# Low-rank weight products in one f16 pass, fewer weight maxima in batch 1, and four banks for its queries and keys

## The chip, the cores and the metric

The kernel runs on one core of a Trainium2 chip. The metric is the device time of one execution in microseconds (us). The engines work on queues of their own and meet at semaphores: TensorE (PE) multiplies matrices into the eight banks of PSUM, VectorE (DVE), ScalarE (ACT) and GpSimd (POOL) do the rest, and SyncE (SP) starts transfers.

## What is computed

The reference is two layers, each added to x (8 batches of 256 tokens, 512 wide).

```python
x = x + ffn0(attention0(x, cond))        # 16 heads; ffn 512 -> 2048 -> 512, relu
x = x + moe1(scan1(cond, x))             # 256 steps of an RK4 scan, then 8 experts, top 2, and a shared expert

w_up = (q - 7.5) * repeat(scale, 64)     # 4-bit codes, one scale for 64
y1 = x1 @ w_up + b_up + x1 @ lora_a @ lora_b        # lora_a [512,16], lora_b [16,2048]
y2 = relu(y1) @ w_down + b_down + relu(y1) @ lora_a2 @ lora_b2   # [2048,16], [16,512]
```

All inputs are f32 but the codes.

## The kernel before

`layer0` does batches 0 to 7 one after the other, `layer1` the scan and the experts. In layer 0 a batch has a stage of queries and keys (its values first), then four quads of four heads, then the product with `w_out`. From batch 2 on, PE does the FFN of batch b-2 in pieces between the attention products; batches 0 and 1 have none.

**Weights of the FFN (batch 0).** The 4-bit weights are made on the chip in 16 pieces of 128x1024 (`PIECES`). For piece h: SP loads codes and scales into one of three stages (it waits for `split` of piece h-3); DVE `unpack` multiplies codes and scales; PE `lora(h)` multiplies the low-rank factors, K = 16, two f32 products of 512 columns, into the banks `D[0]`, `D[1]`; DVE `correct(h)` adds them and counts `stage`; ACT `weights_high(h)` writes the f16 high part, POOL the low part (`split`). The low-rank correction is so folded into the weights. `lora(h)` waits for `stage` of piece h-1, since there is one pair of `D` banks. Pieces 0 to 3 go with the four chunks c of the query and key stage, pieces 4 to 15 with heads 0 to 11 (`lora(h + 4)` stands before `transposed(h)` on PE, `correct(h + 4)` and `unpack(h + 5)` before the copy of `turned(h)` on DVE). Ahead of all, DVE works out the scales (`weight_scales`) and multiplies the factors `lora_up`, `lora_dn` by them, which gives `lora_ok`. `unpack` and `correct` are in DVE's program order, so whatever DVE waits for there holds the head behind it.

**Maxima of the expert weights (batches 1 to 3).** The expert weights of layer 1 are split into f16 parts in batches 4 to 7, and the scale for this needs the largest of them. `part_max(n)` takes one piece of 128x512 (256 KB, loaded by SP into one of four buffers; the load of piece n waits for the maximum of piece n-4). There are 99 pieces, `max_parts(b, at)` deals them to the chunks (4 each) and heads of a batch: 33 to each of batches 1, 2 and 3.

**Queries and keys.** In chunk c PE writes them to `Gb[c % 2]` (banks 0 and 1); ACT squares them, PE sums the squares over a head (`head_norm`, banks `Rb`, 2 and 3), ACT makes 1/sqrt (Ln, Exp) and DVE writes the scaled result (`qk`, counted by `d_qk`). PE begins chunk c >= 2 when `d_qk` of chunk c-2 is there. Banks 6 and 7 (`D`) are idle in batch 1. In a quad PE makes the scores of four heads into banks 0 to 3 (waiting for the last copies, `d_pt`), DVE takes row maxima, ACT Exp, PE transposes, DVE copies back (`turned`), and the next quad's scores follow.

## Time and profile before

| | |
|---|---|
| time, median of 3 runs | 2954.64 us (2946.34 to 2957.25) |
| profiled execution, its own time | 2952.75 us |
| its span in the profile | 2951.0 us |
| PE, DVE, ACT, POOL busy | 95%, 59%, 38%, 46% |
| layer 0, the last largest value of a batch (L857) begins at | 871.3 us |

The busy shares are of the whole span, of which layer 0 is the first three tenths. A stage of layer 0 has its own limits, so the shares say little on this change; the stretches below are named by where they begin and end in us from the span's start.

### The profile page before, as it was taken

Reading aid. Unit: us, or ns where it says so; the run is one execution under the profiler, and the core shown is the slowest. Engines: PE = TensorE matmul, PEld = TensorE weight load, DVE = VectorE, ACT = ScalarE, POOL = GpSimd, SP = SyncE. Lnnn points to the kernel's source line nnn. Section 1 sums busy time; section 2 is a strip of 40 time slices with the busy share of each in tenths; the row PEclk is TensorE's granted clock in tenths of the full one; section 3 lists DMA queues with packets and bytes.
Section 4 is the critical chain, followed back from the end, with each engine's and each line's share of the span. In section 5 each row is a group of like instructions: output and inputs, shape, how many; then the busy total and the mean of one; then the engine's idle time right before and its main releaser. Section 6 shows DMA issues by size and latency. Waiting matters only on the chain.

```text
span 2951.0 us, 133155 instructions
## 1 busy us (share of the span) xinstructions
PE 2793.1 (95%) x49488; PEld 2435.4 (83%) x49488; DVE 1746.9 (59%) x6291; ACT 1125.3 (38%) x4986; POOL 1356.8 (46%) x3466
## 2 busy tenths in 40 slices
PE   7878998998898999999999999999999999999998
PEld 4355776776687778999998999999899899899987
DVE  4645564465464556666666666666666666666654
ACT  2332345456444433333333333333333333333322
POOL 2300001112115666666665666666566566566600
PEclk8578999999999998999999999999999999999999
DMA  7522233344430003444343443444444444344476
GB/s 245 148 79 93 68 106 129 124 147 140 144 100 3 3 4 111 130 129 134 126 130 122 129 131 119 139 129 125 124 130 128 128 130 125 119 138 125 125 232 199
DMA packets 137238, 361.02 MB, mean 122 GB/s; under 512 B 15888, under 2 KB 24720, under 8 KB 136592
## 3 DMA queue, kind: packets, MB, share of 16 engines
q1 hardware_dynamic: 136336, 354.17, 38.2%
q8 instruction: 158, 2.59, 0.4%
q10 hardware_dynamic: 672, 3.67, 0.3%
q14 instruction: 72, 0.59, 0.1%
HBM read 323.31 MB, written 34.47 MB: 121 GB/s over the span
## 4 chain that ended last, share of the span: by engine, by line
PE 59%; POOL 5%; issue 4%; DVE 1%; DMA 0%; ACT 0%; DVEq 0%; POOLq 0%; SPq 0%
PE pscan L1359 12%; PE pg L1264 12%; PE pd L1312 12%; PE pscan L1355 11%; PE pu L1264 11%; POOL lin L1109 1%; POOL lin L1125 0%; POOL from_q L1121 0%; POOL carry L1154 0%; POOL lin L1119 0%; POOL lin L1131 0%; POOL from_q L1127 0%; POOL from_q L1136 0%; POOL lin L1140 0%; PE prouter L1374 0%
## 5 line engine op out<-in xcount | busy, mean ns | idle before, releaser
L1355 PEld LDWEIGHTS pscan<-th,carry 128*128 128x128 f16 x16384 | 552.1, 96 | 73.8 <-ACT th L1174 52.8
L1355 PE MATMUL pscan<-th,carry 128*128 128x8 f16 x16384 | 560.6, 166 | 21.3 <-ACT th L1174 10.6
L1359 PE MATMUL pscan<-th,carry 128*128 128x16 f16 x16384 | 558.4, 169 | 2.2 <-DVE th L1470 1.4
L1359 PEld LDWEIGHTS pscan<-th,carry 128*128 128x128 f16 x16384 | 482.4, 96 | 3.4 <-DVE th L1470 3.3
L1174 ACT ACTIVATE th<-state 128x32 f16<-128x32 f32 x768 | 176.0, 229 | 714.0 <-DVE state L1487 714.0
L1264 PE MATMUL pg<-qh,wbuf 128*128 128x256 f16 x3168 | 432.0, 276 | 14.2 <-issue 14.2
L1312 PE MATMUL pd<-hg,wbuf 128*128 128x256 f16 x3168 | 429.5, 274 | 2.3 <-DMA wbuf<-w_split 2.3
L1264 PE MATMUL pu<-qh,wbuf 128*128 128x256 f16 x3168 | 426.9, 274 | 0.0
L1487 DVE TENSOR_REDUCE state<-pscan 128x32 f32<-128x96 f32 x768 | 197.6, 257 | 270.1 <-PE pscan L1359 264.8
L1264 PEld LDWEIGHTS pg<-qh,wbuf 128*128 128x128 f16 x3168 | 296.5, 98 | 53.9 <-issue 15.5
L1264 PEld LDWEIGHTS pu<-qh,wbuf 128*128 128x128 f16 x3168 | 294.3, 98 | 33.7
L1312 PEld LDWEIGHTS pd<-hg,wbuf 128*128 128x128 f16 x3168 | 278.2, 98 | 32.0 <-issue 2.6
L1482 DVE SCALAR_TENSOR_TENSOR pscan<-pscan,lin 128x32 f32<-128x32 f32 x1024 | 204.4, 200 | 125.1 <-POOL lin L1119 6.6
L1470 DVE TENSOR_TENSOR th<-pact,th 128x32 f16<-128x32 f32 x1024 | 190.7, 186 | 125.9 <-ACT pact L1175 122.8
L1142 POOL TENSOR_TENSOR from_q<-state,carry 128x32 f32<-128x32 f32 x256 | 91.1, 356 | 241.6 <-DVE state L1487 241.6
L1136 POOL TENSOR_TENSOR from_q<-state,carry 128x64 f32<-128x64 f32 x256 | 112.6, 440 | 164.9 <-DVE state L1487 164.9
L1174 ACT ACTIVATE th<-carry 128x32 f16<-128x32 f32 x256 | 58.6, 229 | 329.4 <-DVE carry L1487 323.2
L438 ACT ACTIVATE w_emb<-l0bank,nmax 128x256 f32<-128x256 f32 x256 | 118.8, 475 | 136.9 <-DVE nmax L812 136.9
L292 POOL TENSOR_SCALAR spare<-parts_mem 128x512 f16<-128x512 f16 x33 | 52.0, 1575 | 257.3 <-DMA w_split<-spare 163.6
L1239 ACT ACTIVATE hg<-hp 128x256 f16<-128x256 f32 x264 | 109.7, 416 | 136.3 <-DVE hp L1525 129.6
L310 POOL PARTITION_ALL_REDUCE fs<-fs x8 | 3.0, 378 | 327.3 <-DVE fs L857 327.3
L1525 DVE SCALAR_TENSOR_TENSOR hp<-hb,wk,gates 128x256 f32<-128x256 f32 x264 | 141.0, 534 | 18.7 <-DVE hb L1518 7.6
(231 smaller groups left out, 4928.5 us busy)
## 6 DMA issues: line engine op xcount, KB each, us to landing
wbuf<-w_split SPq DMA_DIRECT2D x264, 512.0 KB, 3.6
wbuf<-w_split SPq DMA_DIRECT2D x264, 384.0 KB, 3.1
parts_mem<-in_w_tiles SPq DMA_DIRECT2D x149, 256.0 KB, 3.1
w_split<-parts_mem SPq DMA_DIRECT2D x99, 256.0 KB, 2.8
late<-in_w_tiles SPq DMA_DIRECT2D x49, 256.0 KB, 3.2
w_split<-spare SPq DMA_DIRECT2D x33, 128.0 KB, 3.0
out<-oo SPq DMA_DIRECT2D x8, 512.0 KB, 3.7
xs<-in_x SPq DMA_DIRECT2D x1, 3584.0 KB, 14.8
```

What stands on the lines that cost most here:

```text
L438: ins = act.activation(pr[:, h % HPC, qc, :], X[h % HPC][:, qc * T:(qc + 1) * T], ACT.Exp, bias=nmax[:, h % HPC, qc:qc + 1], accum_out=psu ...
L1136: pl.tensor_tensor(ms3[:], rows(state[2][:], 2), c3[:], ALU.mult).then_inc(S["pchain"], 1)
L1174: act.activation(th[:, :, 0, :], v3(src[:]), ACT.Tanh, scale=unit).then_inc(S["th_ready"], 1)
L1239: act.activation(hg[:, slot, 0, :], hp[:], ACT.Identity, scale=2.0 ** -11).then_inc(S["hi_ready"], 1)
L1264: ins = mm(dst[:, 0:GT], wgu[:, slot, a, w, k, :], qh[:, q, k, :], start=(k == 0 and w == q), stop=(k == NC - 1 and w == 1))
L1312: ins = mm(pd[m // 2][:, (m % 2) * GT:(m % 2 + 1) * GT], wd[:, slot, w, m * P:(m + 1) * P], hg[:, slot, h, :], start=False, stop=False, sk ...
L1355: mm(pscan[:, 0, m * B:(m + 1) * B], clo[:, k, m * P:(m + 1) * P], th[:, k, 0, :], start=(m == 0 and k == 0), stop=False, skip_group_check ...
L1359: ins = mm(pscan[:, 0:2, m * B:(m + 1) * B], chi[:, k, m * P:(m + 1) * P], th[:, k], start=False, stop=(k == NC - 1), skip_group_check=True)
L1470: dve.tensor_tensor(th[:, :, 1, :], v3(t32), th[:, :, 0, :], ALU.subtract).then_inc(S["tl_ready"], 1)
L1482: chain(dve.scalar_tensor_tensor(pscan[:, 2, 0:W], cub, -RK[s - 1] / 3, A[u][:, s, :], ALU.mult, ALU.add), False)
L1487: dve.tensor_reduce(nxt[:], pscan[:, 0:3, 0:W].rearrange("p a w -> p w a"), AX.X, ALU.add).then_inc(S["q_ready"], 1)
L1525: dve.scalar_tensor_tensor(hp[:], hb[:], wk[:, 4:5], g, ALU.mult, ALU.mult).then_inc(S["hp_ready"], 1)
```

## The change

It has three parts.

1. The low-rank factors come five times stacked over 80 partitions: [a, 0, a, 0, a] and [b, 0, b, 0, b], 16 rows each. They are loaded as f32 into the place of `w_dn` (`stacked`), scaled by powers of two and rounded to f16 by ACT (`factors_high`); DVE `low_of` then puts the rounding remainders into rows 64 to 79 of a and rows 32 to 47 of b. One f16 product with K = 80 is then high x high + high x low + low x high, in place of the f32 product with K = 16. `factors_high(0)` and `low_of(0)` stand ahead of batch 0, `factors_high(1)` and `low_of(1)` (for `w_dn`, pieces 8 to 15) in its chunks 1 and 2. The two loads have 800 KB each, not 160, and the second one stands behind those of pieces 0 and 1.
2. `max_parts`: batches 1, 2 and 3 take 16, 42 and 41 maxima, not 33 each. Those of batch 1 are all in its four chunks (4 each); its heads have none.
3. `gbank`: batch 1 writes chunks 0 to 3 of queries and keys to banks 0, 1, 6 and 7, so that PE doesn't wait for `d_qk`. ACT gets a wait for it instead at chunks 2 and 3, before it overwrites `rh`.

```diff
@@ -133,27 +133,33 @@
...
-        lora_up, lora_dn = late[0:R, 0:N + H0], late[32:32 + R, 0:N + H0]
+        stacked = [w_dn[0:5 * R].rearrange("p a h n -> p (a h n)").bitcast(F32)[:, n * (N + H0):(n + 1) * (N + H0)] for n in range(2)]
+        factors = [late[0:5 * R, n * (N + H0) // 2:(n + 1) * (N + H0) // 2].bitcast(F16) for n in range(2)]
+        fa = [factors[0][:, 0:N], factors[1][:, 0:H0]]
+        fb = [factors[0][:, N:N + H0], factors[1][:, H0:H0 + N]]
...
         largest = spare[:, 0:3 * TILES]
+        power, for_a, for_b = spare[:, 128:130], spare[:, 130:132], spare[:, 132:134]
         bank = [ctx.enter_context(nc.psum_tensor(f"l0bank{i}", [P, 512], F32)) for i in range(8)]
...
         Gb, Rb = X[0:2], X[2:4]
+        def gbank(b, c):
+            return (Gb + D)[c] if isinstance(b, int) and b == 1 else Gb[c % 2]
         first_up = {B - 2: [X[0], X[1]], B - 1: [D[0], Ob[0]]}
...
-        names = ("x_in xs_in emb_in qkv_in wo_in lora vec_in bounds_in coupling_in codes0 codes1 codes2 "
+        names = ("x_in xs_in emb_in qkv_in wo_in lora0 lora1 vec_in bounds_in coupling_in codes0 codes1 codes2 "
                  "eye gch mm_ss amps "
...
                  "chain achain seq plseq "
-                 "mm_lora scaled stage split d_bounds g_bounds lora_ok "
+                 "mm_lora scaled stage split d_bounds g_bounds lora_scale lora_high lora_ok "
                  "part_in0 part_in1 part_in2 part_in3 part_out0 part_out1 part_out2 part_hi part_done part_third third_out widest gmax wscale state_in mx par coef setup").split()
@@ -172,7 +178,8 @@
...
         def max_parts(b, at):
-            return spread((b - 1) * TILES, TILES, at, 4, PARTS) if 1 <= b <= 3 else []
+            first, count = {1: (0, 16), 2: (16, 42), 3: (58, 41)}.get(b, (0, 0))
+            return spread(first, count, at, 4, PARTS) if count else []
         def split_parts(b, at):
@@ -202,10 +209,11 @@
...
             sp.wait_ge(S["qkv_in"], 16)
-            for half, factors in enumerate((lora_up, lora_dn)):
-                sp.dma_start(factors, dram["lora"][half]).then_inc(S["lora"], 16)
+            sp.dma_start(stacked[0], dram["lora"][0]).then_inc(S["lora0"], 16)
             for h in range(PIECES):
                 u = h % 3
+                if h == 2:
+                    sp.dma_start(stacked[1], dram["lora"][1]).then_inc(S["lora1"], 16)
                 if h >= 3:
@@ -376,6 +384,13 @@
...
+            def factors_high(n):
+                act.wait_ge(S["lora_scale"], 1)
+                act.wait_ge(S["lora0"] if n == 0 else S["lora1"], 16)
+                cut = N if n == 0 else H0
+                act.activation(fa[n], stacked[n][:, 0:cut], ACT.Identity, scale=for_a[0:5 * R, n:n + 1])
+                act.activation(fb[n], stacked[n][:, cut:], ACT.Identity, scale=for_b[0:5 * R, n:n + 1]).then_inc(S["lora_high"], 1)
+
             def high(n):
@@ -408,7 +423,7 @@
...
                     act.wait_ge(S["p_qk"], b * NC + c + 1)
-                    act.activation(sqh[:, c % 2], Gb[c % 2][:].rearrange("p (a t) -> p a t", a=2), ACT.Square).then_inc(S["a_sq"], 1)
+                    act.activation(sqh[:, c % 2], gbank(b, c)[:].rearrange("p (a t) -> p a t", a=2), ACT.Square).then_inc(S["a_sq"], 1)
                 def values():
@@ -423,11 +438,15 @@
...
                         act.wait_ge(S["d_x1"], b)
+                    if b == 1 and c >= 2:
+                        act.wait_ge(S["d_qk"], b * NC + c - 1)
                     act.activation(rh[:, c % 2], Rb[c % 2][:].rearrange("p (a t) -> p a t", a=2), ACT.Ln, scale=1.0 / DH, bias=eps).then_inc(S["achain"], 1)
...
                         weights_high(c)
+                    if not b and c == 1:
+                        factors_high(1)
                     relus(ffn_qk[c])
@@ -466,6 +485,7 @@
...
             norm(0)
+            factors_high(0)
             for b in range(B):
@@ -503,17 +523,17 @@
...
             def lora(h):
-                if h == 0:
-                    pe.wait_ge(S["lora_ok"], 1)
-                else:
+                if h % (PIECES // 2) == 0:
+                    pe.wait_ge(S["lora_ok"], h // (PIECES // 2) + 1)
+                if h:
                     pe.wait_ge(S["stage"], h)
...
                     if h < PIECES // 2:
-                        c, col = h // 2, N + h % 2 * PIECE + i * 512
-                        a, bb = lora_up[:, c * P:(c + 1) * P], lora_up[:, col:col + 512]
+                        c, col = h // 2, h % 2 * PIECE + i * 512
+                        a, bb = fa[0][:, c * P:(c + 1) * P], fb[0][:, col:col + 512]
                     else:
                         hc = 2 * (h - PIECES // 2) + i
-                        a, bb = lora_dn[:, hc * P:(hc + 1) * P], lora_dn[:, H0:H0 + N]
+                        a, bb = fa[1][:, hc * P:(hc + 1) * P], fb[1]
                     ins = mm(D[i][:], a, bb, start=True, stop=True)
@@ -563,11 +583,11 @@
...
                 for c in range(NC):
-                    if c >= 2:
+                    if c >= 2 and gbank(b, c) is Gb[c % 2]:
                         pe.wait_ge(S["d_qk"], b * NC + c - 1)
...
                         for k in range(NC):
-                            ins = mm(Gb[c % 2][:, a * T:(a + 1) * T], w_qkv[:, k, a * N + c * P:a * N + (c + 1) * P], xn[:, k, :],
+                            ins = mm(gbank(b, c)[:, a * T:(a + 1) * T], w_qkv[:, k, a * N + c * P:a * N + (c + 1) * P], xn[:, k, :],
                                      start=(k == 0), stop=(k == NC - 1))
@@ -715,14 +735,26 @@
...
                 link(dve.tensor_scalar(swd, fs[:, 14:15], 2.0 ** 13, None, ALU.mult))
+                kp2 = spare[:].bitcast(I32)
+                link(dve.tensor_scalar(power, pairs[:, :, 1], 2.0 ** -60, None, ALU.max))
+                link(dve.tensor_scalar(kp2[:, 128:130], kp2[:, 128:130], 0x7F800000, None, ALU.bitwise_and))
+                link(dve.reciprocal(for_b, power))
+                link(dve.tensor_scalar(for_b, for_b, 0.25, None, ALU.mult))
+                link(dve.scalar_tensor_tensor(for_a, power, 4.0, fs[:, 15:17], ALU.mult, ALU.mult))
+                dve.sem_inc(S["lora_scale"], 1)
                 link(dve.tensor_tensor(kw, fs[:, 11:12], fs[:, 12:13], ALU.mult))
...
                 link(dve.tensor_scalar(b_up, b_up, swu, None, ALU.mult))
-                dve.wait_ge(S["lora"], 32)
-                dve.tensor_scalar(lora_up[:, 0:N], lora_up[:, 0:N], swu[0:R, :], None, ALU.mult)
-                dve.tensor_scalar(lora_dn[:, 0:H0], lora_dn[:, 0:H0], swd[32:32 + R, :], None, ALU.mult).then_inc(S["lora_ok"], 1)
+                low_of(0)
+
+            def low_of(n):
+                dve.wait_ge(S["lora_high"], n + 1)
+                cut = N if n == 0 else H0
+                a, bb = fa[n][4 * R:5 * R], fb[n][2 * R:3 * R]
+                dve.scalar_tensor_tensor(a, stacked[n][4 * R:5 * R, 0:cut], for_a[4 * R:5 * R, n:n + 1], a, ALU.mult, ALU.subtract)
+                dve.scalar_tensor_tensor(bb, stacked[n][2 * R:3 * R, cut:], for_b[2 * R:3 * R, n:n + 1], bb, ALU.mult, ALU.subtract).then_inc(S["lora_ok"], 1)
@@ -799,9 +831,11 @@
...
                         correct(c)
+                        if c == 2:
+                            low_of(1)
                     dve.wait_ge(S["a_hr"], b * NC + c + 1)
-                    dve.scalar_tensor_tensor(qk[:, c, 0, :], Gb[c % 2][:, 0:T], g_q, rh[:, c % 2, 0, :], ALU.mult, ALU.mult)
-                    dve.tensor_tensor(qk[:, c, 1, :], Gb[c % 2][:, T:2 * T], rh[:, c % 2, 1, :], ALU.mult).then_inc(S["d_qk"], 1)
+                    dve.scalar_tensor_tensor(qk[:, c, 0, :], gbank(b, c)[:, 0:T], g_q, rh[:, c % 2, 0, :], ALU.mult, ALU.mult)
+                    dve.tensor_tensor(qk[:, c, 1, :], gbank(b, c)[:, T:2 * T], rh[:, c % 2, 1, :], ALU.mult).then_inc(S["d_qk"], 1)
                     lows(b, ffn_qk[c])
@@ -1624,13 +1658,15 @@
...
     part = lambda a: np.moveaxis(rows(a), 0, 1)
+    gap = np.zeros((R, N + H0), np.float32)
+    stack = lambda m: np.concatenate([m, gap, m, gap, m], 0)
     up_q, dn_q = g("L0_ffn_w_up_q").T, g("L0_ffn_w_down_q").T
...
         "up_q": part(up_q), "dn_q": part(dn_q), "up_s": g("L0_ffn_w_up_scale").T, "dn_s": g("L0_ffn_w_down_scale").T,
-        "lora": np.stack([np.concatenate([g("L0_ffn_w_up_lora_a").T, g("L0_ffn_w_up_lora_b")], 1),
-                          np.concatenate([g("L0_ffn_w_down_lora_a").T, g("L0_ffn_w_down_lora_b")], 1)]),
+        "lora": np.stack([stack(np.concatenate([g("L0_ffn_w_up_lora_a").T, g("L0_ffn_w_up_lora_b")], 1)),
+                          stack(np.concatenate([g("L0_ffn_w_down_lora_a").T, g("L0_ffn_w_down_lora_b")], 1))]),
         "vecs": np.concatenate([part(g("cond_2048").T).reshape(P, NC * B), part(g("L0_cond_b_emb")), part(g("L0_cond_g_norm")),
...
         "b_dn": part(g("L0_ffn_b_down")), "b_scan": part(g("L1_cond_bias")),
```

How this moves the instructions is shown for three places.

DVE ahead of batch 0, before: the last steps of the scales, the factors' two multiplications (`late`), and `unpack` and `correct` of piece 0.

```order
L717 TENSOR_SCALAR fs<-fs 128x1
L718 TENSOR_TENSOR fs<-fs 128x1
L719 TENSOR_SCALAR fs<-fs 128x1
L720 TENSOR_TENSOR fs<-fs 128x1
L721 TENSOR_SCALAR fs<-fs 128x1
L722 TENSOR_SCALAR vecs<-vecs,fs 128x16
L724 TENSOR_SCALAR late<-late,fs 16x512
L725 TENSOR_SCALAR late<-late,fs 16x2048
L731 SCALAR_TENSOR_TENSOR hid<-hid 128x1024
L739 SCALAR_TENSOR_TENSOR hid<-hid,fs,l0bank 128x512 x2
```

The same place after the change, from the row behind the former L717 on (L745 to L749 are the former L718 to L722, L756 and L757 are `low_of`, which waits for ACT; `unpack` follows).

```order
L739 TENSOR_SCALAR spare<-fs 128x2
L740 TENSOR_SCALAR spare<-spare 128x2
L741 RECIPROCAL spare<-spare 128x2
L742 TENSOR_SCALAR spare<-spare 128x2
L743 SCALAR_TENSOR_TENSOR spare<-spare,fs 128x2
L745 TENSOR_TENSOR fs<-fs 128x1
L746 TENSOR_SCALAR fs<-fs 128x1
L747 TENSOR_TENSOR fs<-fs 128x1
L748 TENSOR_SCALAR fs<-fs 128x1
L749 TENSOR_SCALAR vecs<-vecs,fs 128x16
L756 SCALAR_TENSOR_TENSOR late<-w_dn,spare,late 16x512
L757 SCALAR_TENSOR_TENSOR late<-w_dn,spare,late 16x2048
```

Five small steps are new, and the two multiplications have become two subtractions of products that stand behind a wait for ACT.

PE in the query and key stage of batch 1, before (L570 queries and keys, L562 `head_norm`).

```order
L570 MATMUL l0bank0<-carry,w_qkv 128x256 x8
L570 MATMUL l0bank1<-carry,w_qkv 128x256 x8
L562 MATMUL l0bank2<-carry,headones 128x512 [waits l0_a_sq]
L570 MATMUL l0bank0<-carry,w_qkv 128x256 [waits l0_d_qk]
L570 MATMUL l0bank0<-carry,w_qkv 128x256 x7
L562 MATMUL l0bank3<-carry,headones 128x512 [waits l0_a_sq]
L570 MATMUL l0bank1<-carry,w_qkv 128x256 [waits l0_d_qk]
L570 MATMUL l0bank1<-carry,w_qkv 128x256 x7
L562 MATMUL l0bank2<-carry,headones 128x512 [waits l0_a_hr,l0_a_sq]
L562 MATMUL l0bank3<-carry,headones 128x512 [waits l0_a_hr,l0_a_sq]
```

And after (L590 and L582 are the same two lines).

```order
L590 MATMUL l0bank0<-carry,w_qkv 128x256 x8
L590 MATMUL l0bank1<-carry,w_qkv 128x256 x8
L582 MATMUL l0bank2<-carry,headones 128x512 [waits l0_a_sq]
L590 MATMUL l0bank6<-carry,w_qkv 128x256 x8
L582 MATMUL l0bank3<-carry,headones 128x512 [waits l0_a_sq]
L590 MATMUL l0bank7<-carry,w_qkv 128x256 x8
L582 MATMUL l0bank2<-carry,headones 128x512 [waits l0_a_hr,l0_a_sq]
L582 MATMUL l0bank3<-carry,headones 128x512 [waits l0_a_hr,l0_a_sq]
```

The order is the same, and both waits for `d_qk` are gone.

DVE in the first quad of batch 1, before (L812 row maxima, L825 copies, L744 maxima of expert weights).

```order
L812 TENSOR_REDUCE nmax<-l0bank2 128x2
L825 COPY carry<-l0bank0 128x512
L744 TENSOR_REDUCE spare<-parts_mem 128x1
L812 TENSOR_REDUCE nmax<-l0bank3 128x2
L825 COPY carry<-l0bank1 128x512
L744 TENSOR_REDUCE spare<-parts_mem 128x1
L825 COPY carry<-l0bank2 128x512
L744 TENSOR_REDUCE spare<-parts_mem 128x1
L815 RECIPROCAL rinv<-psum_e 128x8
L825 COPY carry<-l0bank3 128x512
L744 TENSOR_REDUCE spare<-late 128x1
```

And after (L846, L859, L849).

```order
L846 TENSOR_REDUCE nmax<-l0bank2 128x2
L859 COPY carry<-l0bank0 128x512
L846 TENSOR_REDUCE nmax<-l0bank3 128x2
L859 COPY carry<-l0bank1 128x512
L859 COPY carry<-l0bank2 128x512
L849 RECIPROCAL rinv<-psum_e 128x8
L859 COPY carry<-l0bank3 128x512
```

The four maxima of the quad are gone; they stand in the heads of batches 2 and 3.

## Rows read from the trace of the kernel before

**Rows 1.** Windows: start:end us, length, busy us (instructions) of each engine, clock, DMA share, GB/s

```profile
32.00:50.00 18.00, 17.24 (x62) 11.15 (x61) 8.03 (x12) 6.32 (x9) 5.89 (x2) 1.00 0.37 101
59.90:87.30 27.40, 16.88 (x49) 6.98 (x48) 15.70 (x21) 9.47 (x22) 10.03 (x5) 0.60 1.00 283
87.30:140.40 53.10, 46.63 (x172) 21.20 (x172) 30.11 (x44) 17.39 (x45) 16.24 (x8) 0.56 0.41 120
165.40:199.60 34.20, 25.19 (x93) 16.52 (x92) 14.36 (x28) 9.77 (x15) 4.03 (x5) 0.99 0.24 76
199.60:255.10 55.50, 40.47 (x297) 27.11 (x298) 37.33 (x67) 18.63 (x71) 0.00 (x0) 0.70 0.37 110
255.10:354.60 99.50, 93.52 (x769) 74.13 (x768) 58.18 (x104) 38.70 (x110) 4.03 (x5) 1.00 0.28 88
354.60:456.60 102.00, 95.00 (x770) 75.04 (x769) 59.04 (x106) 38.80 (x110) 4.03 (x5) 0.98 0.29 86
```

**Rows 2.** Waits of DVE from 87.3 to 140.4: us in total, times, longest

```profile
DVE hid L739 <- PE l0bank L517: 10.5, 5, 2.9
DVE parts_mem L739 <- PE l0bank L517: 5.5, 3, 2.1
```

**Rows 3.** Timeline of one slot of batch 0: start us, us, engine, line, operation

```profile
127.21 0.33 SPq L219 DMA_DIRECT2D hid<-in_dn_q  x1
127.59 2.39 SPq L222 DMA_DIRECT2D hid<-in_dn_s  x4
...
127.76 1.41 DVE L739 SCALAR_TENSOR_TENSOR hid<-hid,fs,l0bank 128x512 f32<-128x512 f32 x2 [1.54 <-PE l0bank L517]
129.09 1.22 DVE L731 SCALAR_TENSOR_TENSOR parts_mem<-parts_mem 128x1024 f32<-128x1024 int32 x1
129.20 1.06 ACT L377 ACTIVATE w_dn<-hid 128x1024 f16<-128x1024 f32 x1 [1.92 <-DVE hid L739]
...
129.22 3.78 PE L517 MATMUL l0bank<-late 16*128 16x512 f32 x4 [0.46 <-DVE hid L739]
130.22 0.68 DVE L825 COPY carry<-l0bank 128x512 f32<-128x512 f32 x1
...
130.34 2.12 POOL L286 TENSOR_TENSOR w_dn<-hid,w_dn 128x1024 f16<-128x1024 f32 x1 [3.15 <-ACT w_dn L377]
```

**Rows 4.** Transfers issued from 127 to 130: issues, KB, median us to landing

```profile
hid<-in_dn_s SPq DMA_DIRECT2D x4, 128.0 KB, 3.7
```

**Rows 5.** Timeline, a low part on POOL earlier in batch 0

```profile
52.54 2.95 POOL L286 TENSOR_TENSOR w_up<-parts_mem,w_up 128x1024 f16<-128x1024 f32 x1 [3.92 <-ACT w_up L377]
```

**Rows 6.** Timeline, 12 f16 products of 256 columns at two clocks

```profile
397.73 2.58 PE L531 MATMUL l0bank<-late,w_up 128*128 128x256 f16 x12
...
400.59 1.47 PE L531 MATMUL l0bank<-late,w_up 128*128 128x256 f16 x12
```

**Rows 7.** Timeline of the start: factors scaled, first low-rank product, chunks 2 and 3

```profile
27.53 1.27 DVE L725 TENSOR_SCALAR late<-late,fs 16x2048 f32<-16x2048 f32 x1
...
29.90 1.98 PE L517 MATMUL l0bank<-late 16*128 16x512 f32 x4
...
38.68 3.72 PE L570 MATMUL l0bank<-carry,w_qkv 128*128 128x256 f32 x16 [0.38 <-DVE w_emb L804]
...
45.55 3.72 PE L570 MATMUL l0bank<-carry,w_qkv 128*128 128x256 f32 x16 [0.38 <-DVE w_emb L804]
```

**Rows 8.** Timeline of batch 1, queries and keys to the first row maxima

```profile
182.75 3.72 PE L570 MATMUL l0bank<-carry,w_qkv 128*128 128x256 f32 x16 [2.29 <-DVE w_emb L804]
...
196.35 1.86 DVE L744 TENSOR_REDUCE spare<-parts_mem 128x1 f32<-128x512 f32 x3
...
199.58 2.09 PE L597 MATMUL l0bank<-w_emb 32*128 32x256 f32 x16 [4.43 <-DVE w_emb L804]
...
203.18 1.88 DVE L812 TENSOR_REDUCE nmax<-l0bank 128x2 f32<-128x512 f32 x3
```

**Rows 9.** Timeline of batch 1, one maximum in a head

```profile
217.29 0.68 DVE L744 TENSOR_REDUCE spare<-parts_mem 128x1 f32<-128x512 f32 x1
```

**Rows 10.** Waits of PE from 255.1 to 456.6 (batches 2 and 3)

```profile
PE l0bank L531 <- DVE hid L770: 1.0, 3, 0.6
```

## The prediction

> **What bounds the kernel now.** PE is the busiest engine of the whole, but the three parts touch batches 0 to 3 only, so I read the windows first, by stage [rows 1]. From 255 us on (batches 2 and 3, with FFN work between the attention products) PE is busy 93.5 of 99.5 and 95.0 of 102.0 us: PE is the bound there. Before that it isn't: in batch 0's quads 0 to 2 (59.9 to 140.4) the granted clock is 0.60 and 0.56, and in the heads of batch 1 PE is busy 40.5 of 55.5 us. There the time is set by a chain that goes round PE, DVE and ACT, and what counts is what stands in that chain.
>
> Batch 0 has two kinds of stretch. In quad 0 the DMA engines are busy all the time (share 1.00) [rows 1]: transfers are the bound, and faster products give nothing. In quads 1 and 2 (53.1 us) the DMA share is 0.41, and DVE waits 10.5 + 5.5 = 16.0 us in `correct` for the low-rank products [rows 1, 2]. The timeline of one slot shows it: `lora` 3.78 us, then `correct`, and only when that is done the next `lora` [rows 3].
>
> In batch 1 the reader is to see two things. PE stands 2.29 us before a chunk of queries and keys, waiting for DVE's scaled result of the chunk two before; and DVE, in program order, does four maxima (1.86 us for three) at 196.35 ahead of the last chunk and four more ahead of the row maxima, which begin at 203.18 though the scores began at 199.58 [rows 8].
>
> **Part 1, the low-rank products.** The changed product streams 512 columns once in f16. Twelve f16 products of 256 columns take 2.58 us at the low clock (1.2 GHz) and 1.47 at the high one (2.4 GHz) [rows 6], so two of 512 cost 2.58 x 4/12 = 0.86 and 0.49 us, against 3.78 and 1.98 [rows 3, 7]. K = 80 instead of 16 fills rows of the array and adds no column; no row shows that alone, and I take it at nothing.
>
> Start. Five more small steps on DVE, about 0.2 us each by those around them: 1.0 us. ACT then rounds 80x512 and 80x2048. 1024 columns take 1.06 us [rows 3], so 2560 take 2.65 at most; I take 2.5. DVE does its other five steps (1.0) meanwhile, then `low_of`: 2560 columns at the 1.22 us per 1024 of `unpack` [rows 3], 3.0 us, I take 2.8 less fixed parts. The multiplications that go have 1.27 + 0.5 us [rows 7]. The factors were ready at 28.8; now at 28.8 - 1.7 + 1.0 + (2.5 - 1.0) + 2.8 = 32.4. `lora(0)` began at 29.90 and took 1.98 [rows 7], so PE was free at 31.9; now it is at 32.4 + 0.1 + 0.5 = 33.0. **+1.2 us**, bounds +0.8 and +3 (all 2560 columns a third dearer). It carries through to quad 0, because the load of x, which starts the full DMA stretch, waits on this chain.
>
> Chunks 1 to 3 of batch 0 gain nothing: `lora` lies in the shadow of ACT's Ln and Exp, PE waits 0.38 us for DVE behind it [rows 7]. The second factors (`factors_high(1)`, 2.5 us on ACT; `low_of(1)`, 2.8 on DVE) go into holes of 3 to 4 us on both engines in that stage, since a chunk's period is 6.87 us [rows 7]. If they didn't fit, each would cost about a microsecond. 1.3 MB more to load goes into the stretch from 32 to 50 us, where the DMA share is 0.37 [rows 1]. Zero for both.
>
> Quads 1 and 2. Of the 16.0 us of waits, three things come back. (a) Batch 1's `norm_sum` stands on PE ahead of `lora(10)`: 0.9 us. (b) Loads: after `correct(n)` come ACT 1.06, POOL 2.12, four scale loads whose issue takes 2.4 us, of which the last starts 2.2 after the codes, and 3.7 to landing [rows 3, 4]: 9.1 us, with semaphores 9.7, until `unpack(n+3)` can run. Left alone, DVE would be there earlier: from the end of the quad's first `correct` it has `unpack` 1.13, copy 0.6, the fourth row maximum 0.6, `correct` 1.33, `unpack` 1.13, copy 0.6, `correct` 1.33 = 6.7 us (each from start to start, as in [rows 3]). So DVE waits 3.0 once in a quad; in quad 1 (a) hides 0.9 of it. (c) A second, short one of 0.5 in quad 1. Sum 0.9 + 2.1 + 0.5 + 3.0 = 6.5. Gain 16.0 - 6.5 = **9.5 us**. Upper bound 16.0. Lower bound: POOL's part can take 2.95 [rows 5], twice in each lag, and landing a little more; 2.5 us dearer for each quad, gain 4.5.
>
> POOL's 2.95 or 2.12 for the same form is a lever here. The Trainium skill, SBUF — State Buffer, section SBUF: two separate sides, says that DVE (with two SBUF inputs) and GpSimd take turns on one exclusive port pair, and the loser is blocked for the whole instruction; by it a denser DVE would make every POOL part slow, and the gain would be 4.5. The row of quads 1 and 2 has 2.12, though DVE works beside it there too, and my sum goes by that.
>
> **Part 3, four banks.** From the end of chunk 1 and `head_norm` (182.75 less the wait of 2.29 [rows 8]: 180.4) PE goes on with chunk 2 3.5, `head_norm` 0.9, chunk 3 3.5, two `head_norm` 1.8: 190 us. DVE's chain: chunk 2 scaled at 190.5 to 191.4, four maxima 2.5 (to 193.9), chunk 3 to 194.8, scores at 194.9 instead of 199.58. Then the last four maxima, bound by their loads as before (6.8 us from one group's start to the row maxima, 196.35 to 203.18 [rows 8]): 191.4 + 7.1 = 198.5 instead of 203.18. **-4.6 us.** Bounds -3 (loads slower, now closer together) and -6.9 (one whole period).
>
> **Part 2, maxima.** In batch 1's heads one maximum stands between the copy and the row maximum that the fourth head's Exp needs [rows 9], 0.6 us, and later ones push the last copy; without them that quad's chain is shorter by 1.15 us (then Exp, transposes and copy follow each other directly), the first one by 0.7. 3 x 1.1 + 0.7 = **-4.0 us**. Bounds -2 and -10 (all 17 x 0.6). In batches 2 and 3, 17 more fall on a DVE that is idle 41 of 99.5 and 43 of 102.0 us, beside a busy PE. What waits there is PE for the hidden layer's low part, 1.0 us in three waits [rows 1, 10]; batch 2's head 4 gets a second maximum right ahead of one. **+0.8 us**; bounds 0 and +10 (all 17 on the path).
>
> **Sum.** +1.2 - 9.5 - 4.6 - 4.0 + 0.8 = -16.1. From the profiled execution's own 2952.75 us: 2936.7. The median of the runs is 1.9 higher than it, within what runs differ; I say 2937.
>
> **Rivals.**
> A, the clock stays up in batch 1. Its stage gets denser, and the heads ran at 0.70 [rows 1]. Scores take 2.09 us at the low clock [rows 8] and half of it at the high one, weighted product and transposes likewise, some 3 us a quad; two more quads at the high clock give -6, so 2931. Against it: PE still idles 5 us before the scores.
> B, the loads hold quads 1 and 2 back and the moved maxima cost in batches 2 and 3: batch 0 gains only 4.5 (5 less), and half of the 17 land on the chain (5 instead of 0.8). -16.1 + 5 + 4.2 = -6.9, so 2946. For it: the slow POOL rows, and that PE has next to no slack there.
> C, PE's clock falls in batch 0's query and key stage, where the f16 product takes 1.5 us of work from each 6.87. At the low clock each period has 3.5 + 0.9 us more on the chain, 3 x 4.4, and the values 7: +20, net +4, 2957, which is slower. It decides from 16 us lost, that is, if four fifths of the stage run low. For it: the 0.60 and 0.56 of the quads. Against it: batch 1's stage keeps 0.99 with PE busy 25.2 of 34.2 us, and batch 0's will have 17.2 - 3 x 1.5 = 12.7 of 18 [rows 1], 71% to 74%. The Trainium skill, TensorE: Matmul & The Clock Gate, section What's actually happening, calls the low clock the default that only activity lifts; by it alone C would be likelier. If batch 1's stage fell too, by as much, it would be +28, 2980.
> D, the f16 products change nothing since loads or POOL bound all of batch 0: what stays is +1.2 - 4.6 - 4.0 + 0.8 = -6.6, 2946. For it: quad 0 is that already; against it: the DMA share of 0.41 [rows 1].
>
> **Chances.** My forecast (2931 to 2943) 0.58, A 0.13, B 0.14, D 0.10, C 0.05. 0.5%, about what a measurement of this kernel can tell from no change, is 14.8 us, so the edge is near 2939. Faster: A, three quarters of the forecast, 0.56. Slower by over 0.5%: only C in both stages, 0.03. Same: 0.41. The range takes in A, B and D: 2928 to 2947.
>
> **What would show it.** `lora` pairs of 0.5 to 0.9 us; DVE's waits on them in quads 1 and 2 near 1 us, and new waits of `unpack` for scales of about 3 us a quad; the start of quad 1 about 1 us later than 87.3, quad 3 8 us earlier than 140.4; from the start of chunk 0 of batch 1's queries to its first row maxima 4.6 us less; heads' quads of 9 us instead of 10; PE 93 busy in batch 2 still. Wrong if quad 0 also shrinks, if the clock row of 20 to 60 drops, or if batches 2 and 3 grow.

## The result, and the profile after

The changed kernel takes 2933.32 us, median of 11 runs (2928.92 to 2943.56), the kernel before 2950.19 us (11 runs, 2946.24 to 2957.25) beside it. The ratio is 0.9944, 95% interval 0.9932 to 0.9957: 16.5 us less (12.7 to 20.1), where the sum said 16.1. The profiled execution has a span of 2932.7 us, 18.3 below that of before.

The windows of the changed kernel, by the same stages as in [rows 1] (the columns are the same).

```profile
32.00:50.00 18.00, 12.01 (x50) 8.37 (x48) 9.65 (x12) 6.92 (x10) 2.94 (x1) 1.00 0.64 156
62.95:92.13 29.18, 7.16 (x42) 3.91 (x41) 15.11 (x21) 9.52 (x22) 11.09 (x5) 0.61 0.97 280
92.13:135.50 43.37, 21.98 (x156) 12.77 (x156) 30.55 (x44) 17.32 (x44) 16.58 (x8) 0.66 0.53 146
160.10:189.30 29.20, 24.45 (x93) 16.50 (x92) 14.70 (x29) 9.77 (x15) 4.02 (x5) 1.00 0.29 90
189.30:241.50 52.20, 37.95 (x296) 26.30 (x297) 27.77 (x50) 18.50 (x71) 0.00 (x0) 0.74 0.10 31
241.50:342.30 100.80, 93.73 (x770) 74.22 (x770) 62.72 (x113) 38.74 (x110) 4.02 (x5) 1.00 0.36 110
342.30:441.50 99.20, 93.52 (x769) 74.14 (x768) 62.97 (x114) 38.64 (x110) 4.02 (x5) 1.00 0.35 110
```

Quad 0 is not shorter (29.2 us, before 27.4). Quads 1 and 2 fell from 53.1 to 43.4 us, PE's busy time in them from 46.6 to 22.0. Batch 1's stage fell by 5.0, its heads by 3.3 up to the values of batch 2. Batch 2 grew by 1.2 (from its values' first product to batch 3's, 99.6 to 100.7), batch 3 shrank by 2.7: its clock was 0.98 before and is 1.00 now. From batch 4's values on, which no part touches, it is 2494.4 us before and 2491.2 after; other profiles have 2489.9 to 2499.1 there, so the 3.2 us there, a part of the 18.3, are no effect.

What DVE waits for in quads 1 and 2 (us in total, times, longest), against [rows 2].

```profile
DVE parts_mem L763 <- DMA parts_mem<-in_dn_s: 3.0, 1, 3.0
DVE hid L763 <- DMA hid<-in_dn_s: 2.8, 2, 2.4
```

The 16.0 us for low-rank products are gone, and in their place `unpack` waits 5.8 us for the scales of w_dn. One slot in the timeline, against [rows 3].

```profile
122.95 2.12 POOL L294 TENSOR_TENSOR w_dn<-hid,w_dn 128x1024 f16<-128x1024 f32 x1 [7.06 <-ACT w_dn L385]
...
125.47 2.39 SPq L230 DMA_DIRECT2D hid<-in_dn_s  x4
...
127.08 1.40 DVE L771 SCALAR_TENSOR_TENSOR parts_mem<-parts_mem,fs,l0bank 128x512 f32<-128x512 f32 x2
128.51 1.06 ACT L385 ACTIVATE w_dn<-parts_mem 128x1024 f16<-128x1024 f32 x1 [1.99 <-DVE parts_mem L771]
128.53 1.04 PE L537 MATMUL l0bank<-late 80*128 80x512 f16 x2 [1.16 <-DVE parts_mem L771]
...
129.64 2.12 POOL L294 TENSOR_TENSOR w_dn<-parts_mem,w_dn 128x1024 f16<-128x1024 f32 x1 [0.93 <-ACT w_dn L385]
130.83 2.02 DVE L763 SCALAR_TENSOR_TENSOR hid<-hid 128x1024 f32<-128x1024 int32 x1 [2.35 <-DMA hid<-in_dn_s]
```

The low-rank pair lasts 1.04 us here, at the low clock; PE waits for DVE, no longer DVE for PE. DVE stands 2.35 us before `unpack`, for scales whose issue began only at 125.47, when POOL was done with the piece three earlier.

The start, against [rows 7] (ACT, DVE and PE, in their order).

```profile
30.95 1.99 ACT L392 ACTIVATE late<-w_dn,spare 80x2048 f16<-80x2048 f32 x1
...
33.05 0.74 DVE L756 SCALAR_TENSOR_TENSOR late<-w_dn,spare,late 16x512 f16<-16x512 f32 x1 [1.68 <-ACT late L392]
...
33.81 2.34 DVE L757 SCALAR_TENSOR_TENSOR late<-w_dn,spare,late 16x2048 f16<-16x2048 f32 x1
...
36.20 0.60 PE L537 MATMUL l0bank<-late 80*128 80x512 f16 x2 [2.56 <-DVE late L757]
36.65 3.62 PE L590 MATMUL l0bank<-carry,w_qkv 128*128 128x256 f32 x16
```

DVE waits 1.68 us for ACT, takes 3.0 for the remainders, and PE waits 2.56 for these.

Batch 1, against [rows 8].

```profile
174.78 3.62 PE L590 MATMUL l0bank<-carry,w_qkv 128*128 128x256 f32 x16
178.24 1.02 PE L582 MATMUL l0bank<-carry,headones 128*128 128x512 f32 x2
179.09 3.62 PE L590 MATMUL l0bank<-carry,w_qkv 128*128 128x256 f32 x16
...
191.74 0.69 DVE L776 TENSOR_REDUCE spare<-parts_mem 128x1 f32<-128x512 f32 x1 [1.18 <-DMA parts_mem<-in_w_tiles]
...
192.99 1.88 DVE L846 TENSOR_REDUCE nmax<-l0bank 128x2 f32<-128x512 f32 x3
```

No wait is left between the chunks. The row maxima still stand behind the last four maxima, and these behind their loads (1.18 us).

### The profile page after: what moved, and what is told of

The parts are those of the page before. It is cut to its first block, busy times and chain, and to the rows that moved or that the text cites. A ratio compares the mean times of both kernels' runs of the same rounds, so it can differ in the third digit from the quotient of the medians.

```text
span 2932.7 us, 133108 instructions
## 1 busy us (share of the span) xinstructions
PE 2748.5 (94%) x49456; PEld 2421.6 (83%) x49456; DVE 1750.9 (60%) x6298; ACT 1129.5 (39%) x4990; POOL 1353.4 (46%) x3466
## 4 chain that ended last, share of the span: by engine, by line
PE 60%; POOL 4%; issue 4%; DVE 1%; ACT 0%; DMA 0%; DVEq 0%; POOLq 0%; SPq 0%
PE pscan L1393 12%; PE pg L1298 12%; PE pd L1346 12%; PE pscan L1389 12%; PE pu L1298 11%; POOL lin L1143 0%; POOL carry L1188 0%; POOL lin L1159 0%; POOL lin L1153 0%; POOL from_q L1155 0%; POOL lin L1165 0%; POOL from_q L1161 0%; POOL from_q L1170 0%; POOL lin L1174 0%; PE prouter L1408 0%
## 5 line engine op out<-in xcount | busy, mean ns | idle before, releaser
L1389 PE MATMUL pscan<-th,carry 128*128 128x8 f16 x16384 | 560.7, 166 | 21.4 <-ACT th L1208 11.1
L1552 DVE SCALAR_TENSOR_TENSOR hb<-pu,wk,ha 128x256 f32<-128x256 f32 x264 | 127.6, 483 | 37.4 <-PE pu L1298 19.1
## 6 DMA issues: line engine op xcount, KB each, us to landing
xs<-in_x SPq DMA_DIRECT2D x1, 3584.0 KB, 13.9
```

The source lines that it names most:

```text
L1389: mm(pscan[:, 0, m * B:(m + 1) * B], clo[:, k, m * P:(m + 1) * P], th[:, k, 0, :], start=(m == 0 and k == 0), stop=False, skip_group_check ...
L1552: dve.scalar_tensor_tensor(hb[:], pu[:, 0:GT], wk[:, 1:2], ha[:], ALU.mult, ALU.mult).then_inc(S["hb_ready"], 1)
```

## The experiments

Times are against runs of the kernel before on the same chip. Its medians beside them were 2951.87 us (the four runs of the parts), 2955.96 (`x_early`, `scales_merged`, `lora0_late`, `all_three`) and 2950.81 (the others), so versions of different groups are compared by their ratios. Stretches named below begin and end where PE starts a stage's first product.

**Each part alone.** `p1_products` has only the new products, `p2_maxima` only the moved maxima, `p3_banks` only the banks (with ACT's wait), `p23_no_f16` the last two.

```diff
 p1_products
-            first, count = {1: (0, 16), 2: (16, 42), 3: (58, 41)}.get(b, (0, 0))
-            return spread(first, count, at, 4, PARTS) if count else []
+            return spread((b - 1) * TILES, TILES, at, 4, PARTS) if 1 <= b <= 3 else []
...
-            return (Gb + D)[c] if isinstance(b, int) and b == 1 else Gb[c % 2]
+            return Gb[c % 2]
```

> Part 1 alone (f16 products; maxima and banks as before). My theory: the start of chunk 1 of batch 0 comes 1.6 us later relative to chunk 0, quad 0 stays bound by transfers (28 to 29.5 us), quads 1 and 2 take 22.5 and 21 us instead of 26.6 and 26.4, in all 8 us less than before. Rival 1: the quads' gain depends on nothing else but the clock, and in this run, at another clock, they take 24 to 26 us each, in all 3 us less. Rival 2: parts 2 and 3 carry the whole gain through the clock, and part 1 alone gives no change.

> Part 2 alone (16, 42 and 41 maxima; f32 products, two banks). My theory: the query and key stage of batch 1 as before (27 us from its chunk 0 to the scores), the heads of batch 1 3 to 4 us shorter, batch 2 about 1 us longer, in all 2.5 to 3 us less than before. Rival: each moved maximum costs 0.6 us in batches 2 and 3 as it saved in batch 1, no change, with batch 2 at 103 us or more.

> Part 3 alone (four banks in batch 1; f32 products, 33 maxima in each batch). My theory: chunk 0 to scores in batch 1 takes 22.3 us instead of 27.05, the row maxima begin about 4.5 us earlier, the heads as before, in all 4.5 us less. Rival: the last maxima wait for their loads, which are now closer together, so the row maxima gain under 2 us, and the scores' gain is lost.

> Parts 2 and 3 together (the change with part 1 undone). My theory, parts add up: batch 0 as before, chunk 0 to scores of batch 1 22.3 us, its heads 3 to 4 us shorter, in all 7 to 8 us less than before, so half of the change's 16.5. Rival: the gain is nearly all part 1's, and this one is within 3 us of before.

| | median us | ratio, 95% | quads 1+2 | batch 1, chunk 0 to scores | its scores to w_out | batch 2 |
|---|---|---|---|---|---|---|
| before | - | - | 53.0 | 27.05 | 46.8 | 99.6 |
| products alone | 2943.29 | 0.9973 (0.9961 to 0.9984) | 45.7 | 27.0 | 46.6 | 99.3 |
| maxima alone | 2947.24 | 0.9982 (0.9971 to 0.9992) | 54.6 | 27.05 | 41.0 | 100.5 |
| banks alone | 2950.83 | 0.9992 (0.9980 to 1.0004) | 53.1 | 22.0 | 47.0 | 99.5 |
| maxima and banks | 2939.25 | 0.9959 (0.9944 to 0.9975) | 48.7 | 22.3 | 41.2 | 100.55 |
| all three, the changed kernel | 2933.32 | 0.9944 (0.9932 to 0.9957) | 43.4 | 22.3 | 43.0 | 100.7 |

The runs of before beside the four had a median of 2951.87, so the parts take off 8.0 us (4.7 to 11.5), 5.3 (2.4 to 8.6) and 2.4 (-1.2 to 5.9): 15.7 together, the whole within its error. Each stretch moves only with the part that the prediction gave it to, but for one: quads 1 and 2 of the f32 kernels differ by 6 us among themselves. So `p23_no_f16` is 12.1 us below before where its expectation has 7 to 8 (4.4 of it stand in these quads), and `p2_maxima` 5.3 where it has 2.5 to 3 (its heads gave 5.8, not 3 to 4).

The granted clock goes with that difference. Here are the quads of `p2_maxima` and of `p23_no_f16`, the longest and the shortest with f32 products (columns as in [rows 1]).

```profile
91.60:146.24 54.64, 48.68 (x168) 21.90 (x168) 30.08 (x44) 17.19 (x44) 16.18 (x8) 0.53 0.40 116
90.34:139.01 48.67, 41.29 (x168) 19.29 (x168) 30.12 (x44) 17.41 (x45) 16.35 (x8) 0.64 0.47 130
```

Before and `p3_banks` have 0.56 and 53.0 and 53.1 us, `before_x_early` 0.60 and 50.5. With f16 products the quads don't follow it: `p1_products` 0.65 and 45.7, the changed kernel 0.66 and 43.4. All nine profiles with f16 products have 0.65 to 0.70 there, more than any with f32; whether the products raise it, no run separates. At about the same clock (0.64 and 0.65) the f16 products take 3 to 4 us off these quads (`lora0_late` has 0.65 and 44.4). The banks alone shorten their stretch by 5.1 us though their time shows half of it; that half is within the interval.

**The load of x two pieces earlier.** In quad 0 DVE waits for scales. SP issues the load of x for batches 1 to 7, 3584 KB in one, at 54.91 in the changed kernel, and it takes 13.9 us to land, into that quad (from 62.95 on). In `x_early` it is issued at 27.97 and has landed 25.4 us later, ahead of the quad. `x_early` is the changed kernel, `before_x_early` the kernel before, each with this edit.

```diff
-                if h == 4:
+                if h == 2:
                     sp.dma_start(xv[:, :, 1:
```

> The changed kernel with the load of x for batches 1 to 7 (3.5 MB) issued behind piece 2 instead of piece 4, about 25 us earlier. My theory, quad 0 of batch 0 is bound by transfers: it takes 20 to 22 us instead of 27 to 29, and the whole 6 to 8 us less than the changed kernel. Rival: quad 0 is bound by the chain of DVE and PE like the others and its wait for scales only shows where the slack is; then it stays above 26 us and nothing is gained.

> The kernel before with one edit, the load of x issued two pieces earlier. If quad 0 is bound by transfers whatever the low-rank product costs, it shrinks here as well, but only to where f32 products hold it, near the 26.5 of quads 1 and 2 less little: 24 to 26.5 us instead of 27.5, and the time falls by 1 to 3 us. If the load of x was what it waited for, as in the changed kernel where the edit took 7.8 us off, quad 0 falls to 22 or less and the time by 5 us or more.

DVE's waits in quad 0, first the changed kernel, then `x_early`, then `before_x_early`.

```profile
DVE parts_mem L763 <- DMA parts_mem<-in_up_s: 6.4, 1, 6.4
DVE hid L763 <- DMA hid<-in_up_s: 5.4, 2, 4.3
```

```profile
DVE hid L763 <- DMA hid<-in_up_s: 4.4, 2, 4.1
...
DVE parts_mem L763 <- DMA parts_mem<-in_dn_s: 0.7, 1, 0.7
```

```profile
DVE hid L739 <- PE l0bank L517: 3.5, 2, 2.1
DVE parts_mem L739 <- PE l0bank L517: 1.5, 1, 1.5
...
DVE hid L731 <- DMA hid<-in_up_s: 0.6, 1, 0.6
```

Quad 0 takes 21.4 us in `x_early`, and 22.0 in `before_x_early`, only 0.6 more, though DVE waits 5.0 us for f32 products in it. So the load of x is what it stood behind in both kernels. `x_early` has 2929.66 us, ratio 0.9911 (0.9892 to 0.9931), where the changed kernel has 0.9944 on another chip; the intervals nearly touch, and beside `scales_merged` of its own group, whose quads and waits are those of the changed kernel, it is 5.1 us faster. What the edit gives the changed kernel is not known closer than that. `before_x_early` has 2943.05 us, 0.9976 (0.9961 to 0.9992), 7 us below before (2.4 to 11.5). There the second case of its expectation held.

**Four scale loads as two.** The issue of four scale loads lies in each lag from `correct` to the `unpack` three pieces on. `scales_merged` issues two, of twice the size.

```diff
-                    for a in range(2):
-                        for half in range(2):
-                            sp.dma_start(scales[u][half * 64:half * 64 + 64, a * N:(a + 1) * N],
-                                         dram["dn_s"][2 * (hc + a) + half].partition_broadcast(64)).then_inc(codes_in[u], 16)
+                    rows = dram["dn_s"][2 * hc:2 * hc + 4].rearrange("(a h) n -> h a n", h=2)
+                    for half in range(2):
+                        sp.dma_start(scales[u][half * 64:half * 64 + 64, :].rearrange("p (a n) -> p a n", a=2),
+                                     rows[half].partition_broadcast(64)).then_inc(codes_in[u], 16)
```

> The changed kernel with the four scale loads of a down piece issued as two of double size. My theory, the wait that took the place of the products' is the lag from correct(n) to unpack(n+3), of which four issues are 2.4 us: the lag gets 1.2 us shorter, DVE's waits for scales in quads 1 and 2 go from 5.9 us in all to about 3, quads 1 and 2 together from 43.4 to 40.5 us. Rival: landing of the larger loads grows by as much as the issue shrinks; waits and quads as they are.

The theory failed. The transfers issued in quads 1 and 2 (KB each, median us from issue to landing), in `scales_merged` and then in the changed kernel:

```profile
hid<-in_dn_s SPq DMA_DIRECT2D x8, 256.0 KB, 5.3
...
parts_mem<-in_dn_s SPq DMA_DIRECT2D x4, 256.0 KB, 5.0
```

```profile
hid<-in_dn_s SPq DMA_DIRECT2D x16, 128.0 KB, 4.0
...
parts_mem<-in_dn_s SPq DMA_DIRECT2D x8, 128.0 KB, 3.9
```

The issue got 1.1 us shorter (1.24 instead of 2.38 us for a piece), the landing 1.1 to 1.3 us longer. DVE waits 3.5 + 3.3 us, no less than 3.0 + 2.8, and the two quads take 43.4 us as before the edit. The time is 2934.74 us, 0.9929 (0.9908 to 0.9949).

**The first low-rank product behind chunk 1.** `lora0_late` lets PE go on with chunk 1 while DVE makes the remainders.

```diff
                     ins.then_inc(S["p_qk"], 1)
+                    if opening and c == 1:
+                        lora(0)
                     if c:
                         head_norm(c - 1)
-                    if opening:
+                    if opening and c:
                         lora(c)
```

> The changed kernel with the first low-rank product behind chunk 1's queries and keys on PE. My theory, PE waits 2.6 us for the factors there and all of it is on the path: chunk 1 begins 3.1 us sooner after chunk 0, chunk 2 2.6 us sooner, and the start of the full DMA stretch with it; 2.5 us less in all. Rival: correct(0) now comes late on DVE and takes the gain back in chunk 2, no change.

PE in its timeline:

```profile
25.70 9.21 PE L590 MATMUL l0bank<-carry,w_qkv 128*128 128x256 f32 x32 [3.78 <-DVE carry L812]
34.75 0.60 PE L537 MATMUL l0bank<-late 80*128 80x512 f16 x2
35.19 1.02 PE L582 MATMUL l0bank<-carry,headones 128*128 128x512 f32 x2
...
38.49 3.72 PE L590 MATMUL l0bank<-carry,w_qkv 128*128 128x256 f32 x16 [1.04 <-DVE w_emb L840]
```

The wait of 2.56 us is gone, and chunk 2 comes 12.8 us behind chunk 0 instead of 15.5. The time is 2930.42 us, 0.9914 (0.9894 to 0.9934). In its profile quad 0 takes 24.8 us, where DVE waits 5.4 + 2.9 us for scales and not 6.4 + 5.4; why is open.

**The steps together.** `all_three` has the three edits, `x_and_late` those of `x_early` and `lora0_late`.

> The changed kernel with all three: x loaded behind piece 2, two scale loads for a down piece, the first low-rank product behind chunk 1. By my theory the gains add up: quad 0 20 to 22 us, quads 1 and 2 40.5 us, start 2.6 us less, 11 to 13 us under the changed kernel, about 2921. Rival: with x early the lag of loads binds quad 0 as well and the start's gain is lost there, 6 us under it, 2927.

> The changed kernel with the load of x issued two pieces earlier and the first low-rank product behind chunk 1, and the four scale loads kept. If the two steps add up where each counts (quad 0 at 21.4 us instead of 29.2, chunk 2 at 12.8 us behind chunk 0 instead of 15.5), the time is some 5 us below the changed kernel at least, 2924 to 2928, and quad 0 starts no later than 62 us. If they compete, since an earlier product and an earlier load both bring pieces 2 and 3 under the same transfers (the rival, for which the three edits together spoke with waits for scales in quad 0), chunk 3 or quad 0 grows by the gain: 2929 to 2932, and no better than one of the two alone.

They don't add up: 2931.51 us, 0.9916 (0.9896 to 0.9936), and 2928.12 us, 0.9925 (0.9901 to 0.9948). By these intervals no version is told apart from `x_early` or `lora0_late` alone. What DVE waits for in `x_and_late` from 28 to 67 us:

```profile
DVE hid L765 <- DMA hid<-in_up_s: 6.7, 2, 5.9
```

The wait of 5.9 us for scales now stands in chunk 3, where the changed kernel had none, and the DMA share from 30 to 62 us is 1.03, where it was 0.70. From chunk 3 to quad 0 it takes 16.3 us instead of 12.7. What quad 0 gives (22.05 us) is in part paid ahead of it. Another 1.7 us of this profile are chunk 2's products at a low clock (5.41 us for 3.72), which other profiles have too (last section).

**K of 16 instead of 80.** `high_only` reads only the first 16 rows; the products with the low parts are left out, though the low parts are still made and loaded.

```diff
-                        a, bb = fa[0][:, c * P:(c + 1) * P], fb[0][:, col:col + 512]
+                        a, bb = fa[0][0:R, c * P:(c + 1) * P], fb[0][0:R, col:col + 512]
```

> The changed kernel, whose low-rank products read only the first 16 of the 80 rows: K = 16 instead of 80. It leaves out the two products with low parts; these are still made and loaded. If the rows of the array that a product fills cost nothing, as the prediction had it, pairs take the same 0.6 and 1.0 us, and the time is that of the changed kernel within 2 us. If K costs, pairs are shorter by a third or more, and quads 1 and 2 by 0.3 us for each pair where PE is waited for, 2 us in all.

The group of all 32 low-rank products (busy us, mean ns of one; idle before them), in `high_only` and then in the changed kernel:

```profile
L537 PE MATMUL l0bank<-late 16*128 16x512 f16 x32 | 12.5, 478 | 19.6 <-DVE parts_mem L771 9.3 <-DVE hid L771 8.1 <-DVE late L757 2.2
```

```profile
L537 PE MATMUL l0bank<-late 80*128 80x512 f16 x32 | 11.8, 457 | 23.6 <-DVE parts_mem L771 11.6 <-DVE hid L771 9.4 <-DVE late L757 2.6
```

Five times the rows cost nothing: with 16 rows the mean is no lower (478 ns) than with 80 (457, and 441 in the second profile of the changed kernel). The time is 2932.32 us, 0.9940 (0.9918 to 0.9962), that of the changed kernel.

**The changed kernel once more.**

> The changed kernel once more, unchanged, for one look at the start. If the slow first products (the 64 of the embedding take 13.8 us, where the f32 kernels have 10.7 to 11.3) belong to the change, they take 13 us or more here too. If it is chance from execution to execution, they take 11 to 12, and chunk 0 starts near 25.5 instead of 27.9.

One more execution took 2944.81 us, span 2943.1, 10.4 us more than the first profile's; 7.9 of them lie behind batch 4's values, which no part touches. The 64 products of the embedding, first in it, then in the kernel before with x early, then in `x_and_late`:

```profile
L520 PE MATMUL l0bank<-vecs,w_emb 128*128 128x8 f32 x64 | 13.6, 357 | 2.6 <-DMA w_emb<-in_w_emb 2.6
```

```profile
L500 PE MATMUL l0bank<-vecs,w_emb 128*128 128x8 f32 x64 | 13.8, 361 | 0.2 <-DMA w_emb<-in_w_emb 0.2
```

```profile
L520 PE MATMUL l0bank<-vecs,w_emb 128*128 128x8 f32 x64 | 10.7, 311 | 0.0
```

By the first row alone the slow start would seem to belong to the change. The other two show that it need not: 13.8 us occurs with the f32 products too, and 10.7 with the f16 ones. Whether the change makes it more frequent is not shown (13.6 to 13.8 us in one of five profiles with f32 products and in six of nine with f16 ones).

In this execution quad 1 took 25.1 us where the first profile has 22.4, with the same program. The trace shows where most of that comes from. POOL and DVE here:

```profile
114.15 2.12 POOL L294 TENSOR_TENSOR w_dn<-parts_mem,w_dn 128x1024 f16<-128x1024 f32 x1 [4.23 <-ACT w_dn L385]
114.54 2.81 DVE L763 SCALAR_TENSOR_TENSOR hid<-hid 128x1024 f32<-128x1024 int32 x1 [1.56 <-DMA hid<-in_dn_s]
```

`unpack` comes 0.39 us behind POOL's low part and takes 2.81 us instead of 1.22. In the first profile the same `unpack` begins 0.7 us ahead of POOL and takes 1.22. It is so in all nine profiles with f16 products: in the three where POOL was first (`after_again`, `p1_products`, `high_only`; 2.81 to 2.95 us) quad 1 takes 24.9 to 25.2 us, in the other six 22.4 to 23.7, while quad 2 takes 20.6 to 20.9 in all.

## Why the prediction was right, and where its steps were off

**Quads 1 and 2: 9.5 us predicted.** The profiled pair shows 9.7 (26.6 + 26.4 to 22.4 + 20.9, predicted 22.6 and 20.9), and the new wait for scales is where it was expected: 3.0 + 0.5 us in quad 1 and 2.35 in quad 2, 5.8 together, where the working has 2.1 + 0.5 and 3.0. That agreement is in part luck. Over five kernels with f32 products the two quads take 48.7 to 54.6 us, mean 52.0; over the four with f16 products and no reordering (the changed kernel twice, products alone, K of 16) 43.4 to 45.8, mean 45.1, and over all nine profiles with f16 products 44.3. The term is rather 7 to 8 us. The mechanism stands; the profile of before was at the long side of what the clock makes of these quads, and the changed kernel's at the short side of what `unpack` and POOL do. A pair of products took 0.60 and 1.04 us, not 0.49 and 0.86, which is not on the path. POOL's parts had 16.58 us for 8 in the two quads, before 16.24, so the lower bound, which went by 2.95 each, wasn't reached.

The prediction read its rows on POOL wrongly. That POOL's 2.12 us stood with "DVE works beside it there too" says nothing against the lock, for what DVE did there was a copy out of PSUM (130.22); `unpack`, both of whose inputs lie in SBUF, had ended at 130.31, before POOL began at 130.34. Where POOL took 2.95 us [rows 5], `unpack` had begun just ahead of it:

```profile
52.28 1.21 DVE L731 SCALAR_TENSOR_TENSOR hid<-hid 128x1024 f32<-128x1024 int32 x1
52.54 2.95 POOL L286 TENSOR_TENSOR w_up<-parts_mem,w_up 128x1024 f16<-128x1024 f32 x1 [3.92 <-ACT w_up L377]
```

In the fourteen profiles an `unpack` and a low part overlap 106 times in batch 0. Where `unpack` came first (80 times), POOL ended 2.0 to 2.1 us after it, whatever the overlap; where POOL came first (26 times), `unpack` ended 1.1 to 1.2 us after POOL. Without an overlap they take 1.22 and 2.12 us (a low part of 2.55 stands beside another DVE operation with two inputs in SBUF, `carry` at L776 of the kernel before), and beside `correct`, which reads PSUM, both keep their times (127.08 and 126.59 in the changed kernel: 1.40 and 2.12 us). The rule in the Trainium skill, SBUF — State Buffer, section SBUF: two separate sides, that VectorE (with two SBUF inputs) and GpSimd lock each other out for a whole instruction, agrees with these traces. So which of the two is longer depends on which starts first.

In quads 1 and 2 of the f32 kernels every `unpack` takes 1.22 us. With f16 products it waits for scales instead and falls into POOL's time: the seven of them take 0.9 us more in the changed kernel's profile, 2.6 more in its second. The working left this out, and it is a part of what the quads gave less.

**The start: +1.2.** The factors came with 0.7 + 2.0 us on ACT and 0.7 + 2.3 on DVE, near the 2.5 and 2.8 taken. From chunk 0 to chunk 1 it takes 8.7 us, before 7.1: +1.6. But the step "chunks 1 to 3 of batch 0 gain nothing" failed for the last of them. `lora(3)` stands on PE directly ahead of the values, where nothing waits: before, the values began 1.9 us after it, now 0.43. From chunk 0 to quad 0 it is 35.2 us before and 35.0 after. The start and this cancel, and the term is 0 by this pair, not +1.2; the other f32 profiles have 37.4 to 38.1 us, 1.7 of them a chunk at the low clock, so it may be nearer -1. The 3.2 us by which chunk 0 itself began later in the profile are for the most part the embedding's, above.

**Quad 0: no gain.** Right, and so was the reason, that transfers bound it, but not complete: it isn't the sum of all bytes, it is one load that stood ahead of the scales. Issuing it earlier gave 5.4 us in the f32 kernel's quad and 7.8 in the changed one's, by single profiles; the quad takes 25.5 to 29.2 us in the five f16 profiles that have neither early x nor the late first product, and against their mean of 27.4 it is 6.0.

**Banks: -4.6.** Chunk 0 to scores fell by 4.8 (27.05 to 22.3), in the two other kernels with banks alone or with the maxima by 5.1 and 4.8. The first row maxima come 30.65 us after chunk 0 before and 25.97 after, 4.7 less. The loads of the last four maxima didn't take it back.

**Maxima: -4.0 in batch 1's heads, +0.8 later.** From the scores to `w_out` it is 3.8 less in the profile (its first three quads 10.9, 10.0 and 8.3 us, before 11.5, 10.6 and 9.9), 5.4 less in the second one, and 5.8 less in `p2_maxima` and `p23_no_f16` against before and `p3_banks`. Over all fourteen profiles the mean is 46.7 without and 41.7 with the moved maxima, 4.9 less; so the term was too small by 0.9. In batches 2 and 3, 17 maxima more cost 1.1 us in batch 2 (100.5 to 100.7 in the kernels of the table that have them and in the changed kernel's second profile, 99.3 to 99.6 without) and nothing in batch 3 (99.3 to 100.0 with, 99.4 to 99.9 without, leaving out the profile of before, whose clock fell there). PE's waits for the hidden layer's low part rose from the 1.0 us of [rows 10]:

```profile
PE l0bank L551 <- DVE hid L802: 2.2, 4, 0.8
```

**The rivals.** A: the clock of batch 1's heads is 0.74, before 0.70, so they did not stay at the high clock. B: batch 0 gained more than 4.5, and the moved maxima cost 1, not 5. C: the changed kernel has 1.00 from 32 to 50 us. In five of the nine f16 profiles the clock fell for one stretch of the query and key stage, but in four of the five f32 ones too (last section), so this is not the change's and costs 1.7 us, in one profile (`high_only`) 3.8, not 20. D: the products alone take off 8.0 us. The end is right because the terms are near theirs, with a start that is 1 to 2 us cheaper, quads that give some 2 us less, and heads that give 0.9 more.

## What to carry to other kernels

A product on a ring of engines is worth what the next link of the ring allows: work out when the next buffer comes free, and the gain follows (16 us of waits, 3 us a quad given back to loads). A stretch with a DMA share of 1.0 isn't for that bound by bytes; look at which single load stands ahead of the one waited for: moving one line was worth about as much here (7 us with f32 products) as the whole low-rank part (8). Before another engine's operation is moved, see what it will run beside: here a wait that only changed its cause put `unpack` into POOL's time and cost up to 2.6 us. Two reorderings that each free the same transfers do not add up, and a single profile of each kernel tells such stretches only to 3 us.
